# Value stages of two attention layers: spread values on ScalarE, half of the keys added on POOL, h added on TensorE

## The chip, the cores and the metric

The kernel runs on one NeuronCore of a Trainium2 chip. The metric is device time of one execution in microseconds (us). Engines are named as in the profile: PE is TensorE (PEld its weight loads), DVE is VectorE, ACT is ScalarE, POOL is GpSimd, SP is SyncE. All tensors here are float32.

## What is computed

A small vision tower over 128 images: patch embedding with window attention (9 patches and a class token), then attention, a mixture of experts, attention again, and a low-rank mixture. The change touches the two attentions. Cut to what matters, each is

```python
# x: layernorm(h); h is [128 images, 10 tokens, 256 channels], 16 heads of 16
q, k, v  = x @ Wq.T, x @ Wk.T, x @ Wv.T        # layer 0 with biases
scores   = einsum('bhqd,bhkd->bhqk', q, k) / 4
# layer 0: entries (0, 9) and (9, 0) set to -1e9; layer 1: clipped to +-10, then causal mask
weights  = softmax(scores)
out      = einsum('bhqk,bhkd->bhqd', weights, v)
h        = h + out @ Wo.T
```

So token t has `t + 1` keys in layer 1, and all 10 in layer 0.

## The kernel before

**Tiling.** The 128 images lie on the 128 partitions. A token is a tile `t` of 256 columns (T = 10, C = 256), so that attention runs inside a partition and none of it is a matmul between tokens. `h` holds 10 such tiles (`h_at(t)`). `a_qkv[:, t, :]` holds query, key and value of tile t, 256 columns each.

**Scores.** For each query the products with all keys are made by DVE or POOL and summed over 16 channels by DVE; ACT takes the exponent into `a_p`, with layout (query, head, key). `softmax_half` (DVE) divides: weights for POOL's queries stay in `a_p` (SBUF), those for DVE's queries go into a PSUM bank (`weight_bank`).

**The value stage**, once a layer. For each query t the values of n keys (`keys(layer, t)`: 10 in layer 0, t + 1 in layer 1) are multiplied with the weights and added over the keys. Queries are split by engine: `POOL_VALUES` (0, 2, 4, 6, 8 in layer 0; 0, 1, 2, 3, 4, 6, 8 in layer 1) and `DVE_VALUES` (the others).
- DVE's queries: `value_products` (line 1158) writes the products with the key innermost, n x 4 bytes apart from one channel to the next, from values that lie with the channel innermost; then a reduction over the last axis gives `a_o` (line 1469). TensorE turns `a_o` (`turn`, line 300).
- POOL's queries: `value_products` (the same line 1158) writes one row of 256 channels for each key into one of two slots (`pool_slot`). TensorE adds and turns them in one step: for each half of the channels, n matmuls with the unit matrix into one PSUM bank (line 1290). A matmul of float32 shows as two passes in the trace, so ten keys and two halves are 40.

ACT copies the turned result to SBUF (`a_oT`, line 1365). TensorE projects it with Wo (`project_o`, `mm_rows`, line 294, four passes), and DVE adds h (`add_o`, line 1485), then takes the statistics of the next layer norm (lines 347 and 349, and `veps`, line 354).

**Order of the work.** There is no planner: each engine has one instruction stream, and the order is the order in the source. Engines meet at counting semaphores. What matters here:
- PE: `turn_o(t)`, then `project_o(t - 1)`. `project_o(t)` waits for `a_h_made` of tile t - 1 (line 1305), since two banks alternate.
- DVE: products and sum of one of its queries, then `add_o` for the tiles up to t - 4, then the next query; at the end the remaining `add_o`. `add_o` waits for the projection.
- POOL: its queries in order; from the third on it waits until TensorE has turned the query two before in its list. After them come the reciprocal deviations (line 336) for the next stage.
- ACT: in layer 0 two exponents and then the copies `a_oT`; in layer 1 a loop over tiles that normalizes, copies the turned x (line 1323), copies queries, keys and values from PSUM (lines 1327, 1329) and takes the exponent of one query (`row_exponent`, line 1335).

Layer 0 is followed by the expert stage: `norm_rows` (line 364) normalizes h on ACT, TensorE turns it and computes the router's logits, and ranking, gathering and 27 expert slots follow, which TensorE fills. SP loads the experts' weights after the logits. Layer 1 is followed by the low-rank stage. No DMA is issued by the value stages.

## Time and profile before

| | us |
|---|---|
| median of 3 runs | 852.29 |
| lowest and highest | 847.16, 853.20 |
| the profiled execution, its own time | 849.13 |
| its span, first to last instruction | 847.4 |
| mean granted clock of TensorE in it | 0.931 |
| PE busy (4399 instructions) | 729.8, 86% |
| DVE busy | 535.9, 63% |
| POOL busy | 396.5, 47% |
| ACT busy | 358.6, 42% |

All times inside the kernel are of that one profiled execution, counted from the start of its span. In it the first value stage lies between about 430 and 489 us and the second between about 784 and 819. Busy shares are of the whole span; stages have different limits. The granted clock is a share of 2.4 GHz: 1.00 is the high of its two levels (2.4 GHz) and 0.50 the low one (1.2 GHz). An engine's idle time is followed by the one whose signal ended it. Durations of PE passes overlap with those of their neighbours, so a group's time is read from its first start to its last end.

### The profile page before, as it was taken

The page shows a single profiled execution, that of the slowest core. Times are in us where ns is not written, and L with a number is a line of the kernel's source. Part 1 is how long each engine was busy: PE and PEld are TensorE (multiplying, and loading weights), DVE is VectorE, ACT ScalarE, POOL GpSimd, SP SyncE. Part 2 cuts the span into 40 slices and gives each one's busy share as a digit, 9 for nine tenths or more (in the row PEclk, how much of TensorE's full clock was granted, in tenths as well). Part 3 has the DMA queues.
Part 4 walks back from the last instruction along what each step waited for, and adds up shares of the span by engine and source line. Part 5 has one row for each costly group of instructions (what it writes and reads, how often), then busy time and mean ns, then how long its engine had stood idle before and what let it go on. Part 6 is the DMA issues. An engine that isn't in the chain of part 4 may idle for free.

```text
span 847.4 us, 13115 instructions
## 1 busy us (share of the span) xinstructions
PE 729.8 (86%) x4399; PEld 630.6 (74%) x4399; DVE 535.9 (63%) x1253; ACT 358.6 (42%) x904; POOL 396.5 (47%) x272
## 2 busy tenths in 40 slices
PE   2879999999999999996846755999999999595668
PEld 2869998988989887553645754999999999354666
DVE  1578787777777777678999653222222223679956
ACT  3465666656656555532010131444444444162131
POOL 4565767667576661548564202333334332147410
PEclk9899999999999999999958865999999999597999
DMA  8532222222222020000020047799989980400001
GB/s 257 174 91 81 86 87 86 81 60 76 87 86 84 4 100 1 0 1 0 1 100 1 26 174 298 239 339 325 332 331 331 330 327 28 160 0 2 0 1 63
DMA packets 34489, 102.76 MB, mean 121 GB/s; under 512 B 3624, under 2 KB 12152, under 8 KB 27000
## 3 DMA queue, kind: packets, MB, share of 16 engines
q1 hardware_dynamic: 31832, 94.84, 32.6%
q0 software_dynamic: 2592, 7.10, 2.2%
q8 instruction: 36, 0.59, 0.3%
q14 instruction: 29, 0.24, 0.1%
HBM read 95.75 MB, written 6.17 MB: 120 GB/s over the span
## 4 chain that ended last, share of the span: by engine, by line
PE 69%; DVE 20%; POOL 3%; DMA 2%; issue 2%; ACT 1%; SPq 1%; POOLq 1%; DVEq 0%; ACTq 0%
PE banks L1581 12%; PE banks L1589 11%; PE banks L287 10%; PE banks L289 10%; PE banks L288 10%; PE banks L294 6%; PE banks L300 4%; DVE a_prod L1158 4%; PE banks L1260 4%; DVE a_o L1469 2%; DVE a_s L1393 2%; DVE banks L1393 1%; DVE w_raw L1402 1%; PE banks L1290 1%; PE banks L1919 1%
## 5 line engine op out<-in xcount | busy, mean ns | idle before, releaser
L401 POOL TENSOR_TENSOR x_lo<-xraw,x_hi 128x640 fp32r<-128x640 f32 x81 | 129.3, 1603 | 109.8 <-ACT x_hi L395 109.8
L287 PE MATMUL banks<-wc_hi,x_hi 128*128 128x256 f32 x405 | 121.9, 301 | 17.9 <-POOL x_lo L401 12.6
L1679 ACT ACTIVATE hid<-banks,b 128x128 f32<-128x128 f32 x216 | 79.3, 367 | 110.0 <-PE banks L1581 110.0
L288 PE MATMUL banks<-wc_lo,x_hi 128*128 128x256 f32 x405 | 116.5, 288 | 0.0
L289 PE MATMUL banks<-wc_hi,x_lo 128*128 128x256 f32 x405 | 116.4, 287 | 0.0
L287 PEld LDWEIGHTS banks<-wc_hi,x_hi 128*128 128x128 f32 x405 | 79.5, 196 | 20.4 <-issue 12.9
L1838 DVE TENSOR_TENSOR res<-banks,xb 128x256 f32<-128x256 f32 x27 | 11.5, 425 | 127.2 <-PE banks L1589 127.2
L288 PEld LDWEIGHTS banks<-wc_lo,x_hi 128*128 128x128 f32 x405 | 79.7, 197 | 1.8 <-issue 0.2
L289 PEld LDWEIGHTS banks<-wc_hi,x_lo 128*128 128x128 f32 x405 | 79.3, 196 | 0.0
L424 DVE BATCH_NORM_STATS2 stats<-banks 128x6 f32<-128x256 f32 x81 | 34.6, 427 | 69.7 <-ACT pe_sb L418 69.0
L418 ACT ACTIVATE pe_sb<-banks 128x256 f32<-128x256 f32 x81 | 31.0, 383 | 111.8 <-PE banks L289 111.8
L287 PE MATMUL banks<-wkv_hi,xg_hi 128*128 128x512 f32 x162 | 70.9, 438 | 4.4 <-DVE xg_lo L485 4.2
L1581 PEld LDWEIGHTS banks<-xT,w_raw 128*128 128x128 f32 x448 | 67.8, 196 | 5.8 <-ACT xT L1667 0.9
L1581 PE MATMUL banks<-xT,w_raw 128*128 128x128 f32 x448 | 69.6, 280 | 0.5 <-ACT xT L1667 0.5
L1717 POOL TENSOR_TENSOR y<-bve,mhalf 128x1 f32<-128x1 f32 x27 | 20.4, 755 | 104.9 <-DVE bve L1846 104.9
L1290 PE MATMUL banks<-ident,a_prod 128*128 128x128 f32 x324 | 46.5, 311 | 24.4 <-POOL a_prod L1158 24.4
L336 POOL TENSOR_TENSOR rstd<-veps,mhalf 128x5 f32<-128x5 f32 (+5 forms) x31 | 32.6, 1053 | 73.7 <-DVE veps L354 57.0
L1589 PE MATMUL banks<-w_raw,hid 128*128 128x256 f32 x224 | 66.9, 380 | 0.0
L1290 PEld LDWEIGHTS banks<-ident,a_prod 128*128 128x128 f32 x324 | 46.2, 227 | 25.9 <-issue 15.6
L1581 PEld LDWEIGHTS banks<-xT,w1more 128*128 128x128 f32 x416 | 61.8, 191 | 4.7
L289 PE MATMUL banks<-wkv_hi,xg_lo 128*128 128x512 f32 x162 | 64.5, 398 | 0.0
L288 PE MATMUL banks<-wkv_lo,xg_hi 128*128 128x512 f32 x162 | 63.9, 395 | 0.0
(298 smaller groups left out, 1778.5 us busy)
## 6 DMA issues: line engine op xcount, KB each, us to landing
w_raw<-in_w SPq DMA_DIRECT2D x28, 1024.0 KB, 6.7
xraw<-in_x_main SPq DMA_DIRECT2D x27, 768.0 KB
w1more<-in_w SPq DMA_DIRECT2D x13, 1024.0 KB, 5.8
w2more<-in_w SPq DMA_DIRECT2D x13, 1024.0 KB, 8.2
xraw<-in_x_rest SPq DMA_DIRECT2D x27, 114.0 KB
yl<-y_rows SPq DMA_DIRECT2D x2, 1028.0 KB, 7.1
a_w<-in_qkv_w SPq DMA_DIRECT2D x2, 768.0 KB, 5.4
x_rows<-w_raw SPq DMA_DIRECT2D x5, 256.0 KB, 2.0
```

The lines of the kernel that those rows point to most:

```text
L287: pe.matmul(dst, a[0], b[0], start=start, stop=False)
L288: pe.matmul(dst, a[0], b[1], start=False, stop=False)
L289: return pe.matmul(dst, a[1], b[0], start=False, stop=stop)
L294: last = pe.matmul(dst, aT[:, c * P:(c + 1) * P], w[:, c, a:b], start=(c == 0), stop=(c == CH - 1))
L300: last = pe.transpose(dst[:, c * P:(c + 1) * P], src[:, c * P:(c + 1) * P], ident[:, :])
L401: pool.tensor_tensor(x_lo[:, i % RING_X, :], xraw[:, k].rearrange("p c b -> p (c b)"), x_hi[:, i % RING_X, :], ALU.subtract).then_inc(sem( ...
L424: dve.bn_stats(stats[0][:, k, :], bank(i % 2)).then_inc(sem("stats_made0"), 1)
L1158: return eng.tensor_tensor(out, a_qkv[:, 0:n, 2 * C:3 * C].rearrange("p s (h d) -> p s h d", d=D16), key_weights(layer, t, n), ALU.mult)
L1290: last = pe.matmul(bank(t % 2, c * P, (c + 1) * P), slot[:, k * C + c * P:k * C + (c + 1) * P], ident[:, :], start=(k == 0), stop=(k == ns ...
L1581: last = pe.matmul(bank(fc % 2, 0, P), weights_of(s)[0][:, c * FF + fc * P:c * FF + (fc + 1) * P], xT[:, s % 2, c * P:(c + 1) * P], start= ...
L1589: last = pe.matmul(down_bank(s), hid[:, s % 2, fc, :], weights_of(s)[1][:, fc * C:(fc + 1) * C], start=(fc == 0), stop=(fc == FC - 1))
L1679: act.activation(hid[:, s % 2, fc, :], bank(fc % 2, 0, P), ACT.Gelu, bias=b1[:, bass.ds(e * FC + fc, 1)]).then_inc(sem("gelu_made"), 1)
```

## The change

- ACT gets a new piece of work, `spread_values`: it copies the values from `a_qkv` into `a_prod[:, 1, :]` with the key innermost (`values_by_channel`: channel c, key s at column 10 c + s). In layer 0 this is one copy of 2560 elements behind the two exponents, in layer 1 one of 256 elements for each tile, in the loop; there the exponents move one round later, and the last spread stands between the exponents of queries 8 and 7.
- DVE's products (`dve_values`) read values, and write products, both with the key innermost. DVE has one slot in place of two (`a_prod[:, 0]`) and waits for its own sum of the query before, and once for all spreads.
- POOL, where a query has more than five keys, adds the upper part of its rows to the lower part (`fold_pool_values`): ten keys leave five in layer 0; in layer 1 query 6 has seven and leaves four, query 8 has nine and leaves five. TensorE sums only what is left (`kept_keys`).
- `project_o` has a third matmul, unit matrix by `h_at(t)`, into the same bank. DVE's addition to h goes; ACT copies the bank into h (`copy_h(t - 1)` behind the copy of `a_oT` for tile t) and signals `a_h_made`.
- Two semaphores take over the counts of two others (`unfolded` those of `vprod_raw`, `consts_made` that of `a_p_cleared`).

The diff, cut to its core:

```diff
+        def pool_values(pool, layer, t):
             n = keys(layer, t)
+            p_t = a_p[:, t * T * H16:(t + 1) * T * H16].rearrange("p (h s) -> p s h", s=T)[:, 0:n, :]
+            return pool.tensor_tensor(pool_slot(layer, t)[:, 0:n * C].rearrange("p (s h d) -> p s h d", s=n, d=D16),
+                                      a_qkv[:, 0:n, 2 * C:3 * C].rearrange("p s (h d) -> p s h d", d=D16),
+                                      p_t.unsqueeze(3).broadcast_to([P, n, H16, D16]), ALU.mult)
+        def kept_keys(layer, t):
+            n = keys(layer, t)
+            return (n + 1) // 2 if n > HALF else n
+        def folded(layer, t):
+            return kept_keys(layer, t) < keys(layer, t)
+        def fold_pool_values(pool, layer, t):
+            n, m = keys(layer, t), kept_keys(layer, t)
+            slot = pool_slot(layer, t)
+            return pool.tensor_tensor(slot[:, 0:(n - m) * C], slot[:, 0:(n - m) * C], slot[:, m * C:n * C], ALU.add)
+        def values_by_channel(n=T):
+            return a_prod[:, 1, :].rearrange("p (c s) -> p c s", s=T)[:, :, 0:n]
+        def dve_values(dve, layer, t):
+            n = keys(layer, t)
+            i = [q for q in DVE_VALUES[layer] if q // HALF == t // HALF].index(t)
+            p_t = weight_bank(t // HALF, i * T * H16, (i + 1) * T * H16).rearrange("p (h s) -> p h s", s=T)[:, :, 0:n]
+            return dve.tensor_tensor(a_prod[:, 0, 0:n * C].rearrange("p (h d s) -> p h d s", h=H16, s=n),
+                                     values_by_channel(n).rearrange("p (h d) s -> p h d s", d=D16),
+                                     p_t.unsqueeze(2).broadcast_to([P, H16, D16, n]), ALU.mult)
...
+                if folded(layer, t):
+                    pool_values(pool, layer, t).then_inc(sem("unfolded"), 1)
+                    pool.wait_ge(sem("unfolded"), NW + 1 + made)
+                    fold_pool_values(pool, layer, t).then_inc(sem("a_pool_values_made"), 1)
+                else:
+                    pool_values(pool, layer, t).then_inc(sem("a_pool_values_made"), 1)
...
-                ns, slot = keys(layer, t), pool_slot(layer, t)
+                ns, slot = kept_keys(layer, t), pool_slot(layer, t)
...
-                mm_rows(pe, bank(6 + t % 2), a_oT[:, t % 2, :], wo, 0, C).then_inc(sem("a_o_done"), 1)
+                for c in range(CH):
+                    pe.matmul(bank(6 + t % 2), a_oT[:, t % 2, c * P:(c + 1) * P], wo[:, c, :], start=(c == 0), stop=False)
+                pe.matmul(bank(6 + t % 2), ident[:, :], h_at(t), start=False, stop=True).then_inc(sem("a_o_done"), 1)
...
+        def spread_values(act, layer, a, b):
+            act.wait_ge(sem("a_qkv_made"), seen(layer, "qkv_made", 2 * b))
+            act.activation(values_by_channel()[:, :, a:b].rearrange("p c s -> p s c"), a_qkv[:, a:b, 2 * C:3 * C], ACT.Copy)\
+               .then_inc(sem("a_values_spread"), 1)
+        def copy_h(act, layer, t):
+            act.wait_ge(sem("a_o_done"), seen(layer, "o_done", t + 1))
+            act.activation(h_at(t), bank(6 + t % 2), ACT.Copy).then_inc(sem("a_h_made"), 1)
...
                     if t:
                         copy_qkv(act, 1, t - 1)
-                    if t >= 4:
-                        row_exponent(act, SCORED[t - 4])
+                        spread_values(act, 1, t - 1, t)
+                    if t >= 5:
+                        row_exponent(act, SCORED[t - 5])
                 copy_qkv(act, 1, T - 1)
-                for t in SCORED[T - 4:]:
+                for t in SCORED[T - 5:T - 2]:
+                    row_exponent(act, t)
+                spread_values(act, 1, T - 1, T)
+                for t in SCORED[T - 2:]:
                     row_exponent(act, t)
...
+                spread_values(act, 0, 0, T)
...
                 act.activation(a_oT[:, t % 2, :], bank(t % 2), ACT.Copy).then_inc(sem("a_oT_made"), 1)
+                if t:
+                    copy_h(act, layer, t - 1)
                 if layer == 0 and t == 7:
                     norm_rows(act, 0)
+            copy_h(act, layer, T - 1)
...
+            dve.wait_ge(sem("a_values_spread"), 1 + T * layer)
             for i, t in enumerate(DVE_VALUES[layer]):
...
-            dve.wait_ge(sem("a_o_done"), seen(layer, "o_done", t + 1))
-            dve.tensor_tensor(h_at(t), bank(6 + t % 2), h_at(t), ALU.add).then_inc(sem("a_h_made"), 1)
             dve.wait_ge(sem("a_h_made"), seen(layer, "h_made", t + 1))
```

## Rows read from the trace of the kernel before

**Rows 1.** Time by stretch, value stages: us, busy time by engine, PEclk, DMA.

```profile
430.30:488.50 58.20, 40.93 (x256) 38.07 (x256) 51.17 (x48) 6.18 (x15) 25.76 (x7) 0.79 0.11 42
...
784.40:818.70 34.30, 21.95 (x143) 19.95 (x141) 28.30 (x41) 3.06 (x8) 12.47 (x5) 0.95 0.00 0
```

**Rows 2.** Chain that ended last, first value stage (start us, us, what).

```profile
433.56 4.76 DVE a_prod L1158
438.34 2.82 DVE a_o L1469
...
479.38 5.66 PE banks L1290 x40
...
488.57 0.92 ACT w_raw L364 x2
```

**Rows 3.** Waits of the first value stage (us in total, times, longest).

```profile
PE banks L294 <- DVE h L1485: 12.1, 3, 6.9
```

**Rows 4.** Groups of POOL by shape (xcount, busy us, mean ns, idle before).

```profile
L1158 POOL TENSOR_TENSOR a_prod<-a_qkv,a_p 128x2560 f32<-128x2560 f32 x5 | 23.7, 4755 | 20.3 <-PE banks L1290 15.2 <-DVE a_p L1435 5.0
...
L1117 POOL TENSOR_TENSOR a_prod<-a_qkv 128x1280 f32<-128x1280 f32 x1 | 2.9, 2905 | 0.0
...
L604 POOL TENSOR_TENSOR vprod<-vprod 128x1024 f32<-128x1024 f32 x10 | 24.0, 2400 | 0.7
```

**Rows 5.** Order of time, POOL and DVE, first value stage (start us, us).

```profile
430.39 9.46 POOL L1158 TENSOR_TENSOR a_prod<-a_qkv,a_p 128x2560 f32<-128x2560 f32 x2 [5.03 <-DVE a_p L1435]
...
464.61 4.75 POOL L1158 TENSOR_TENSOR a_prod<-a_qkv,a_p 128x2560 f32<-128x2560 f32 x1 [11.03 <-PE banks L1290]
...
467.69 1.69 DVE L354 TENSOR_SCALAR veps<-mv 128x4 f32<-128x4 f32 x1
```

**Rows 6.** Groups of DVE by shape, from 400 to 490 us.

```profile
L1158 DVE TENSOR_TENSOR a_prod<-a_qkv,banks 128x2560 f32<-128x2560 f32 x5 | 23.7, 4731 | 0.0
...
L1402 DVE TENSOR_TENSOR w_raw<-a_qkv,banks 128x2560 f32<-128x2560 f32 x1 | 2.8, 2820 | 0.0
```

**Rows 7.** Order of time, PE, first value stage.

```profile
435.26 7.34 PE L1290 MATMUL banks<-ident,a_prod 128*128 128x128 f32 x40 [15.32 <-POOL a_prod L1158]
...
444.05 4.63 PE L1290 MATMUL banks<-ident,a_prod 128*128 128x128 f32 x40
...
485.96 1.89 PE L294 MATMUL banks<-a_wo,a_oT 128*128 128x256 f32 x8
```

**Rows 8.** Groups of ACT by shape, whole run.

```profile
L1365 ACT ACTIVATE a_oT<-banks 128x256 f32<-128x256 f32 x20 | 7.6, 383 | 75.7 <-PE banks L1290 70.8 <-PE banks L300 4.9
...
L1335 ACT ACTIVATE a_p<-a_s 128x160 f32<-128x160 f32 x1 | 0.5, 489 | 4.6 <-DVE a_s L1388 4.6
...
L1335 ACT ACTIVATE a_p<-a_s 128x16 f32<-128x16 f32 x1 | 0.2, 233 | 0.0
```

**Rows 9.** Order of time, ACT, layer 1's query, key and value loop.

```profile
753.46 1.28 ACT L1335 ACT_TABLE_LOAD   x1
...
760.60 0.60 ACT L1327 ACTIVATE a_qkv<-banks 128x512 f32<-128x512 f32 x1 [0.67 <-PE banks L1260]
761.46 0.38 ACT L1329 ACTIVATE a_qkv<-banks 128x256 f32<-128x256 f32 x1 [0.27 <-PE banks L1260]
```

**Rows 10.** Chain that ended last, second value stage.

```profile
784.45 2.97 DVE a_prod L1158
...
808.33 4.02 PE banks L1290 x36
...
818.75 2.07 ACT z_xn L364 x4
```

**Rows 11.** Order of time, POOL, second value stage.

```profile
787.21 3.37 POOL L1158 TENSOR_TENSOR a_prod<-a_qkv,a_p 128x1792 f32<-128x1792 f32 x1 [0.17 <-PE banks L1290]
...
793.16 4.28 POOL L1158 TENSOR_TENSOR a_prod<-a_qkv,a_p 128x2304 f32<-128x2304 f32 x1 [2.58 <-PE banks L1290]
```

**Rows 12.** Time by stretch, two us with TensorE nearly idle.

```profile
787.00:789.00 2.00, 0.07 (x1) 0.00 (x0) 1.97 (x2) 0.38 (x1) 1.83 (x2) 1.00 0.00 0
```

More of the change, by code:

```diff
@@ L599, in value_prod @@
                                by_key(attn).unsqueeze(3).broadcast_to([P, NP, H8, DH8]), ALU.mult)\
-                .then_inc(sem("vprod_raw"), 1)
+                .then_inc(sem("unfolded"), 1)
         def fold_values(pool, n):
-            pool.wait_ge(sem("vprod_raw"), n + 1)
+            pool.wait_ge(sem("unfolded"), n + 1)
             pool.tensor_tensor(vprod[:, C:KEPT * C], vprod[:, C:KEPT * C], vprod[:, KEPT * C:], ALU.add).then_inc(sem("vprod_made"), 1)
@@ L1145, in score_place @@
                 "p h s -> p s h" if kind == "row" else "p s h -> p s h")
-        def key_weights(layer, t, n):
-            if t in DVE_VALUES[layer]:
-                i = [q for q in DVE_VALUES[layer] if q // HALF == t // HALF].index(t)
-                p_t = weight_bank(t // HALF, i * T * H16, (i + 1) * T * H16)
-            else:
-                p_t = a_p[:, t * T * H16:(t + 1) * T * H16]
-            return p_t.rearrange("p (h s) -> p s h", s=T)[:, 0:n, :].unsqueeze(3).broadcast_to([P, n, H16, D16])
@@ L1156, in value_products @@
-        def value_products(eng, layer, t, out):
-            n = keys(layer, t)
-            return eng.tensor_tensor(out, a_qkv[:, 0:n, 2 * C:3 * C].rearrange("p s (h d) -> p s h d", d=D16),
-                                     key_weights(layer, t, n), ALU.mult)
+        def pool_values(pool, layer, t):
+            n = keys(layer, t)
+            p_t = a_p[:, t * T * H16:(t + 1) * T * H16].rearrange("p (h s) -> p s h", s=T)[:, 0:n, :]
+            return pool.tensor_tensor(pool_slot(layer, t)[:, 0:n * C].rearrange("p (s h d) -> p s h d", s=n, d=D16),
+                                      a_qkv[:, 0:n, 2 * C:3 * C].rearrange("p s (h d) -> p s h d", d=D16),
+                                      p_t.unsqueeze(3).broadcast_to([P, n, H16, D16]), ALU.mult)
@@ L1177, in pool_slot @@
             return a_prod[:, 2 + POOL_VALUES[layer].index(t) % 2, :]
-        def dve_slot(layer, t):
-            return a_prod[:, DVE_VALUES[layer].index(t) % 2, :]
         def job_place(layer, i):
@@ L1205, in pool_attention @@
                 inverse_std(pool, *batch_of("attention 1", 0))
-                pool.memset(a_p[:, :], 0.0).then_inc(sem("a_p_cleared"), 1)
+                pool.memset(a_p[:, :], 0.0).then_inc(sem("consts_made"), 1)
                 inverse_std(pool, *batch_of("attention 1", 1))
@@ L1211, in pool_attention @@
             for i, t in enumerate(POOL_VALUES[layer]):
-                n = keys(layer, t)
                 pool.wait_ge(sem("a_p_made"), seen(layer, "p_made", 1 + t // HALF))
@@ L1215, in pool_attention @@
                     pool.wait_ge(sem("a_o_turned"), seen(layer, "o_turned", POOL_VALUES[layer][i - 2] + 1))
-                value_products(pool, layer, t, pool_slot(layer, t)[:, 0:n * C].rearrange("p (s h d) -> p s h d", s=n, d=D16))\
-                    .then_inc(sem("a_pool_values_made"), 1)
+                made = sum(folded(0, q) for q in POOL_VALUES[0]) * layer + sum(folded(layer, q) for q in POOL_VALUES[layer][:i + 1])
+                if folded(layer, t):
[4 more added lines that the diff above has]
+                    pool_values(pool, layer, t).then_inc(sem("a_pool_values_made"), 1)
             if layer == 0:
@@ L1329, in copy_qkv @@
             act.activation(a_qkv[:, t, 2 * C:3 * C], bank(5), ACT.Copy).then_inc(sem("a_qkv_made"), 1)
+        def spread_values(act, layer, a, b):
[5 more added lines that the diff above has]
+            act.activation(h_at(t), bank(6 + t % 2), ACT.Copy).then_inc(sem("a_h_made"), 1)
         def row_exponent(act, t):
-            act.wait_ge(sem("a_p_cleared"), 1)
+            act.wait_ge(sem("consts_made"), 5)
             act.wait_ge(sem("a_s_made"), seen(1, "s_made", SCORED.index(t) + 1))
@@ L1462, in dve_attention @@
             added = 0
+            dve.wait_ge(sem("a_values_spread"), 1 + T * layer)
             for i, t in enumerate(DVE_VALUES[layer]):
-                n, slot = keys(layer, t), dve_slot(layer, t)
-                by_key = slot[:, 0:n * C].rearrange("p (h d s) -> p s h d", s=n, d=D16)
-                if i >= 2:
-                    dve.wait_ge(sem("a_o_made"), len(DVE_VALUES[0]) * layer + i - 1)
-                link(value_products(dve, layer, t, by_key))
-                dve.tensor_reduce(a_o[:, t * C:(t + 1) * C], slot[:, 0:n * C].rearrange("p (c s) -> p c s", s=n), AX, ALU.add)\
+                n = keys(layer, t)
+                if i:
+                    dve.wait_ge(sem("a_o_made"), len(DVE_VALUES[0]) * layer + i)
+                link(dve_values(dve, layer, t))
+                dve.tensor_reduce(a_o[:, t * C:(t + 1) * C], a_prod[:, 0, 0:n * C].rearrange("p (c s) -> p c s", s=n), AX, ALU.add)\
                    .then_inc(sem("a_o_made"), 1)
```

## The prediction

> **What bounds the kernel now.** I first read the windows of the profile by stage, to see how full each engine is in the two value stages [rows 1]. In the first (58.2 us) DVE is busy 51.2, TensorE 40.9 and POOL only 25.8; in the second (34.3 us) DVE is busy 28.3 and POOL 12.5. Then I read the chain that ended last, to see which engine sets the end. In the first stage it is DVE without a gap: five times a product of 4.76 us and a sum of 2.82, with h additions and statistics between them, and only then TensorE's last forty passes (ended 485.04) and the tail to ACT's normalization at 488.57 [rows 2]. Third, the waits: TensorE waits 12.1 us in all for DVE's additions to h, since project_o(t) needs h(t-1) and the additions queue behind DVE's products [rows 3]. POOL waits in turn for TensorE (15.2 us before its products) to free a slot [rows 4]. So DVE is the bound, and the other two engines idle behind it.
>
> **The first value stage (layer 0), part by part.** POOL keeps its product of 4.76 us [rows 4] and gains a fold of five keys, 5 x 256 = 1280 elements. The trace has no such fold there. A POOL product of 1280 elements takes 2.905 us, and a POOL fold of 1024 takes 2.400, which scales to 3.0 [rows 4]; a fold for nothing is excluded, because both rows read two SBUF tensors at that rate. I take 2.95, and 7.75 a tile with the wait between the two. POOL starts at 430.39, as before [rows 5]. Five tiles without a stall end at 430.39 + 38.75 = 469.15. A stall is not due: the third tile needs the first slot back at 445.9, and the first tile is handed over at 438.15.
>
> DVE loses ten h additions. Its product should fall to the price of the score product, which also reads one SBUF and one PSUM tensor, writes in order and takes 2.82 us for the same 2560 elements, against 4.73 now [rows 6]. The bounds are 2.82 and 4.73; what is different about the old product is its output, written 40 bytes apart, so I take 2.82. DVE then needs about 5.65 us a tile and is ahead of POOL. Even at 4.73 its last tile would come at about 474, some 1 us after TensorE wants it.
>
> TensorE's sums halve, to twenty passes a tile. Forty took 4.63 us at the high clock (0.116 each) and 7.34 at the low one (0.184) [rows 7]. So the last sums start 0.15 after POOL and end at 469.15 + 0.15 + 2.3 = 471.6, in place of 485.04: 13.4 us earlier.
>
> The tail gets longer. project_o has six passes in place of four; eight took 1.89 us [rows 7], so 0.24 each, 1.4 a tile. From the end of the last sums to the end of project_o(9) it is now 3 x 1.4 = 4.2 us. Then ACT copies h (9) and turns x2(0), which are queued ahead of the normalization, 0.38 each with little overlap [rows 8]; with them and the hand-over it starts 4.85 after the sums. Before it started 488.57 - 485.04 = 3.53 after them [rows 2]. Loss 1.3. POOL's next reciprocal deviations wait for its last fold, until 469.15, and ACT's first four normalizations then end near 472.3, just before they would hold up the copy for tile 8. **Gain of the first stage: 13.4 - 1.3 = 12.1 us.**
>
> ACT's spread: its exponent writes 40 bytes apart too, 0.489 us for 160 elements and 0.233 for 16 [rows 8], so 1.78 ns an element. The spread of 2560 is then 0.2 + 4.55 = 4.75 us, and it starts behind the exponents, some 4.6 us before DVE's first product at 433.56 [rows 2]; the two come out even to within 0.2. Cost nothing: DVE is not the bound any more and has some 5 us to spare.
>
> One more wait moves. DVE's veps took 1.69 us, from 467.69 until 469.38, and POOL's product ended at 469.36 [rows 5]: DVE stood until POOL had let go. POOL is now busy without a break, so the veps after tile 3 may stand for a whole fold, up to 2.95 us. DVE's slack of 5 us hides it. The Trainium skill says on the page "SBUF — State Buffer", section "Who interferes with whom", that a DVE instruction in a two-port mode, or one with two SBUF inputs against a reading POOL instruction, blocks outright for that instruction; by this rule, the trace agrees on veps, and the sum stays as it is.
>
> **The second value stage (layer 1).** Two things differ. First, ten small spreads of 256 elements stand in ACT's loop for queries, keys and values, 0.2 + 240 x 1.78 ns = 0.66 us each. In a round ACT waits 0.67 and 0.27 us for TensorE [rows 9], 0.94 together, so a spread fits. But round 5 also has the table load of 1.28 us [rows 9], and 0.66 + 1.28 do not fit into 0.94: query 6, which DVE waits for, comes 1.0 us late (0 to 1.5). From there DVE is full, so the stage starts at 785.45 in place of 784.45 [rows 10].
>
> Second, only tiles 6 and 8 are folded (three and four keys). POOL's product of tile 6 began at 787.21, when TensorE had summed tile 3 [rows 11]; that is now 1.0 later for the start and 0.9 for two longer projections: 789.1. Then product 3.37 and fold 1.85, product 4.28 [rows 11] and fold 2.4 [rows 4], with hand-overs 12.1: 801.2. Twenty passes follow, to 803.6. Before, the thirty-six ended at 808.33 + 4.02 = 812.35 [rows 10], so 8.75 earlier. DVE (tiles 5, 7, 9 at 1.75 + 1.75, 2.3 + 2.3, 2.8 + 2.8, and six statistics) is done with tile 9 at 801.5, ahead. The tail up to ACT's normalization was 6.4 us [rows 10] and grows by only 0.2, since h(9) comes later but no addition queues in DVE. **Gain: 8.5 us.**
>
> Between and behind the stages nothing else changes, and the experts, which start from the routing, move forward with it. The renamed semaphores cost nothing.
>
> **Sum.** 12.1 + 8.5 = 20.6 us. The profiled execution took 849.13 us (span 847.4), which gives 828.5. I add 1.5 for TensorE at the low clock in parts where it was at the high one (0 to 11, below): 830.0. The median of the runs is 852.29, 3.2 above the profiled execution; against it 830 is 2.6% less. A difference of about 1% is what a measurement of this kernel can tell.
>
> **The rivals.** *TensorE falls to the low clock in both tails.* The mean was 0.79 of full speed in the first stage and 0.95 in the second [rows 1], and TensorE now has less to do. Then twenty passes cost 1.4 us more and 4.2 us of projections up to 4.2 more: 5.5 a stage, 11 in all, 839.5. Against it: its idle time before the last sums is some 2.4 and 2 us, and a stretch of 2 us with TensorE almost idle still shows 1.00 [rows 12], while the forty slow passes came after 15.3 us of idling [rows 7]. The Trainium skill, page "TensorE: Matmul & The Clock Gate", Part 1, holds that low is the default and that activity lifts it; the trace agrees in the slow passes after the long idle time, and by it this rival is what a thinner TensorE gets. Chance 0.15.
>
> *DVE's product stays at 4.7 us*, since the order of writing was not its cost. Tile 9 comes 1 to 2 us late in either stage: 833. Chance 0.06.
>
> *POOL and DVE shut each other out.* If the new DVE product held what POOL reads through, 5 x 2.82 = 14 us would go onto POOL's path in the first stage and 5 in the second: a loss of 2 and a gain of 3.4, 848. Against it: POOL's products take 4.755 us on average beside DVE's present ones [rows 4], and the new one has its weights in PSUM as well. Chance 0.03.
>
> *Slower: the spread is dear on ACT.* Say s us for 256 elements. In layer 1 ten of them stretch the loop by 10(s - 0.9); in layer 0 the one spread takes 10s, and above s = 1.3 DVE's last tile is late by 10s - 13.2. Gains of 20.6 (with the 1.0 in it) are used up at s = 2.2, and s = 3 gives about 866. The exponent's rows give 0.66 [rows 8]. Chance 0.03.
>
> **How the numbers follow.** The forecast, POOL as the pace of both stages, has 0.73 and a range of its own of 824 to 836 (the runs of before lie 6 us apart; the fold is 2.9 to 3.0, the late query 0 to 1.5, the clock 0 to 5). With the clock rival whole the range is 822 to 840. Faster by over 1% (below 843.8): 0.73 + 0.15 + 0.06 = 0.94, less 0.02 for what I have not seen, 0.92. Within 1%: 0.05. Slower: 0.03.
>
> **What would show it.** After: POOL in the first stage busy 38 us without a gap, folds of 2.9 us; DVE products of 2.8 us; the last sums ending 38 to 42 us after POOL's first product; no wait of TensorE for h; the wait that ends last before TensorE's sums is POOL's. Each spread of 256 at 0.66 us, and the value stage of layer 1 starting about 1 us later behind its loop. The forecast is wrong if POOL's products become longer beside the folds, if the passes of the tails take 0.18 us and more, or if POOL waits for TensorE again.

## The result and the profile after

| | before | after |
|---|---|---|
| median, us | 850.87 (4 runs, 847.16 to 853.20) | 828.34 (4 runs, 827.10 to 829.73) |
| ratio, 95% interval | | 0.9745 [0.9718, 0.9771] |
| profiled execution | 849.13 | 829.73 |
| its span | 847.4 | 827.6 |
| mean granted clock | 0.931 | 0.938 |

The changed kernel is 2.5% faster. The forecast was 830.0 with a range of 822 to 840. The kernel before has one run more here than ahead of the prediction, which moved its median from 852.29 to 850.87. Its profiled execution lies 1.7 us below that median, the one of the changed kernel 1.4 above its own, so that the profiles differ by 19.4 us and the medians by 22.5.

**Where the 19.8 us of the span lie.** I cut both profiles at the same instructions. Each number is the difference of two starts.

| stretch | before | after | change | forecast |
|---|---|---|---|---|
| start of the span to POOL's first value product | 430.39 | 431.40 | +1.01 | 0 |
| layer 0: to ACT's second group of normalizations for the expert stage | 58.18 | 45.78 | -12.40 | -12.1 |
| routing: to DVE's comparison that opens the expert slots | 18.54 | 16.79 | -1.75 | 0 |
| experts: to DVE's first addition to h | 225.36 | 225.67 | +0.31 | 0 |
| to DVE's score product of query 6, layer 1 | 28.83 | 29.90 | +1.07 | +1.0 |
| to DVE's first value product of layer 1 | 23.15 | 23.15 | 0 | 0 |
| layer 1: to ACT's first normalization of the low-rank stage | 34.30 | 25.93 | -8.37 | -9.5 |
| rest | 28.65 | 28.98 | +0.33 | 0 |
| span | 847.40 | 827.60 | -19.80 | -20.6, and 1.5 allowed for the clock |

The 8.5 us that the prediction gives for layer 1 are these 9.5 less the 1.0 of query 6.

The windows of the changed kernel by stage (us, then the busy time of PE, PEld, DVE, ACT and POOL, the granted clock, DMA) answer to [rows 1]:

```profile
431.40:477.20 45.80, 31.69 (x176) 27.91 (x176) 37.45 (x38) 12.60 (x27) 40.08 (x12) 0.81 0.13 52
772.70:798.60 25.90, 22.25 (x145) 19.97 (x143) 19.62 (x30) 6.59 (x18) 16.62 (x7) 1.00 0.00 1
```

POOL, busy 25.8 of 58.2 us before, is busy 40.1 of 45.8 in the first stage. The waits of the changed kernel from 430 to 489 us (us in total, times, longest) answer to [rows 3]:

```profile
PE banks L1310 <- POOL a_prod L1165: 24.5, 5, 18.3
...
DVE a_prod L1175 <- ACT a_prod L1356: 0.2, 1, 0.2
```

TensorE's wait for DVE's additions to h (12.1 us before) has no line any more. TensorE now waits for POOL's fold in front of each of its five sums, and DVE waits 0.2 us in all for ACT's spread. The groups of the same stretch by shape (xcount, busy us, mean ns) answer to [rows 4] and [rows 6]:

```profile
L1150 POOL TENSOR_TENSOR a_prod<-a_qkv,a_p 128x2560 f32<-128x2560 f32 x5 | 23.8, 4758 | 5.0 <-DVE a_p L1475 5.0
...
L1165 POOL TENSOR_TENSOR a_prod<-a_prod 128x1280 f32<-128x1280 f32 x5 | 14.5, 2893 | 0.4
...
L1175 DVE TENSOR_TENSOR a_prod<-a_prod,banks 128x2560 f32<-128x2560 f32 x5 | 14.1, 2812 | 0.2 <-ACT a_prod L1356 0.2
...
L1356 ACT ACTIVATE a_prod<-a_qkv 128x2560 f32<-128x2560 f32 x1 | 4.8, 4759 | 0.0
```

DVE's product fell from 4731 to 2812 ns, and POOL's stayed as it was beside it (4755, now 4758). In order of time (start, us), the changed kernel's first stage shows the new path, POOL and then TensorE and then ACT:

```profile
431.40 4.76 POOL L1150 TENSOR_TENSOR a_prod<-a_qkv,a_p 128x2560 f32<-128x2560 f32 x1 [5.02 <-DVE a_p L1475]
...
459.30 2.89 POOL L1165 TENSOR_TENSOR a_prod<-a_prod 128x1280 f32<-128x1280 f32 x1
...
461.20 1.01 DVE L354 TENSOR_SCALAR veps<-mv 128x4 f32<-128x4 f32 x1
...
466.99 2.88 POOL L1165 TENSOR_TENSOR a_prod<-a_prod 128x1280 f32<-128x1280 f32 x1
...
470.02 2.47 PE L1310 MATMUL banks<-ident,a_prod 128*128 128x128 f32 x20 [2.40 <-POOL a_prod L1165]
472.32 1.03 PE L1327 MATMUL banks<-a_wo,a_oT 128*128 128x256 f32 x4
...
471.09 2.08 ACT L364 ACTIVATE w_raw<-h,nmr,rstd 128x256 f32<-128x256 f32 x4 [3.05 <-DVE nmr L341]
473.07 0.36 ACT L1402 ACTIVATE a_oT<-banks 128x256 f32<-128x256 f32 x1
...
477.18 2.07 ACT L364 ACTIVATE w_raw<-h,nmr,rstd 128x256 f32<-128x256 f32 x4
```

POOL's last fold ends at 469.87, 38.47 us after its first start: 7.69 a query. The last sums end at 472.49, 41.09 after it, and ACT's second group starts 4.69 later. In layer 1 the changed kernel's order of time shows the one place that the forecast had not in it:

```profile
770.04 2.07 PE L1327 MATMUL banks<-a_wo,a_oT 128*128 128x256 f32 x4
771.91 1.06 PE L1328 MATMUL banks<-h,ident 128*128 128x256 f32 x2
...
774.50 2.47 POOL L1150 TENSOR_TENSOR a_prod<-a_qkv,a_p 128x1280 f32<-128x1280 f32 x1 [2.35 <-PE banks L1310]
```

The first projection runs at the low clock (2.07 and 1.06 us, later 1.03 and 0.59), and POOL waits 2.35 us for the slot that TensorE sums behind it.

### The profile page after: what moved, and what is told of

The parts are those of the page before. It is cut to its first block, busy times and chain, and to the rows that moved or that the text cites. A ratio compares the mean times of both kernels' runs of the same rounds, so it can differ in the third digit from the quotient of the medians.

```text
span 827.6 us, 12959 instructions
## 1 busy us (share of the span) xinstructions
PE 720.0 (87%) x4311; PEld 618.7 (75%) x4311; DVE 513.3 (62%) x1233; ACT 375.7 (45%) x935; POOL 414.6 (50%) x279
## 4 chain that ended last, share of the span: by engine, by line
PE 71%; DVE 12%; POOL 9%; DMA 2%; ACT 2%; issue 2%; SPq 1%; POOLq 1%; DVEq 0%; ACTq 0%
PE banks L1619 12%; PE banks L1627 11%; PE banks L287 10%; PE banks L289 10%; PE banks L288 10%; PE banks L294 5%; PE banks L300 4%; POOL a_prod L1150 3%; PE banks L1280 2%; POOL a_prod L1165 2%; PE banks L1310 2%; DVE a_s L1433 2%; DVE w_raw L1442 1%; PE banks L1957 1%; DVE banks L1433 1%
## 5 line engine op out<-in xcount | busy, mean ns | idle before, releaser
L287 PEld LDWEIGHTS banks<-wc_hi,x_hi 128*128 128x128 f32 x405 | 79.6, 196 | 21.1 <-issue 13.6
L1619 PE MATMUL banks<-xT,w1more 128*128 128x128 f32 x416 | 63.2, 274 | 0.0
L1280 PE MATMUL banks<-a_w,a_xT 128*128 128x512 f32 (+1 forms) x160 | 61.5, 519 | 0.4 <-DVE w_raw L1442 0.3
L1627 PE MATMUL banks<-w2more,hid 128*128 128x256 f32 x208 | 61.6, 380 | 0.0
```

What stands on the lines that cost most here:

```text
L287: pe.matmul(dst, a[0], b[0], start=start, stop=False)
L1280: last = pe.matmul(dst, a_xT[:, t % 2, c * P:(c + 1) * P], a_w[layer][:, c, a:b], start=(layer == 1 and c == 0), stop=(c == CH - 1))
L1619: last = pe.matmul(bank(fc % 2, 0, P), weights_of(s)[0][:, c * FF + fc * P:c * FF + (fc + 1) * P], xT[:, s % 2, c * P:(c + 1) * P], start= ...
L1627: last = pe.matmul(down_bank(s), hid[:, s % 2, fc, :], weights_of(s)[1][:, fc * C:(fc + 1) * C], start=(fc == 0), stop=(fc == FC - 1))
```

## The experiments

**The theory** is that of the prediction: DVE was the bound, each part of the change takes work off DVE or TensorE until POOL paces the stage, and the parts share one path. **The rival** is that each part is worth its own busy time, so that their gains add. A second question, which the first kernels opened, is what the fold of layer 0 is worth, and why the slow product costs the stage more than the prediction said. The ratios compare each kernel with runs of the kernel before on the same chip; times are medians in us. The medians of the kernel before were 851.03 beside the three kernels without one part and the first with late spreads, 850.89 beside the parts alone, 853.02 beside the repeat of the changed kernel and the three with another fold or none in layer 0, and 850.00 beside the last row. Medians of different sets can thus differ by 1 to 3 us for no reason of the kernels; the ratios are free of that.

| kernel | median | ratio, 95% | layer 0 stage | routing | to query 6 | layer 1 stage |
|---|---|---|---|---|---|---|
| before | 850.87 | | 58.18 | 18.54 | 28.83 | 34.30 |
| changed | 828.34 | 0.9745 [0.9718, 0.9771] | 45.78 | 16.79 | 29.90 | 25.93 |
| changed, once more | 828.49 | 0.9730 [0.9698, 0.9762] | 45.73 | 16.82 | 29.88 | 24.52 |
| without the spread | 832.19 | 0.9777 [0.9740, 0.9814] | 52.25 | 19.22 | 28.84 | 26.62 |
| without h on TensorE | 833.78 | 0.9795 [0.9757, 0.9832] | 44.60 | 18.59 | 29.92 | 30.54 |
| without the folds | 830.94 | 0.9756 [0.9716, 0.9795] | 45.19 | 19.24 | 29.90 | 26.09 |
| spreads of layer 1 late | 827.03 | 0.9728 [0.9686, 0.9770] | 45.76 | 16.95 | 28.83 | 24.97 |
| the spread alone | 833.72 | 0.9805 [0.9786, 0.9824] | 48.16 | 18.68 | 29.91 | 29.58 |
| h on TensorE alone | 837.30 | 0.9853 [0.9832, 0.9874] | 52.27 | 19.28 | 28.81 | 26.75 |
| the folds alone | 847.53 | 0.9965 [0.9945, 0.9984] | 56.19 | 17.14 | 28.81 | 35.32 |
| fold of three keys in layer 0 | 824.96 | 0.9671 [0.9645, 0.9696] | 43.26 | 17.39 | 29.88 | 25.57 |
| the same, spreads late | 825.91 | 0.9692 [0.9669, 0.9715] | 43.25 | 17.35 | 28.82 | 24.61 |
| no fold in layer 0, spreads late | 827.87 | 0.9712 [0.9687, 0.9737] | 45.10 | 19.33 | 28.81 | 25.93 |
| without the spread, one normalization moved | 831.23 | 0.9791 [0.9757, 0.9825] | 48.35 | 18.80 | 28.82 | 26.59 |

The stretches are those of the table above, each from the one profiled execution of its kernel.

### 1. Without the spread

```diff
-            return dve.tensor_tensor(a_prod[:, 0, 0:n * C].rearrange("p (h d s) -> p h d s", h=H16, s=n),
-                                     values_by_channel(n).rearrange("p (h d) s -> p h d s", d=D16),
-                                     p_t.unsqueeze(2).broadcast_to([P, H16, D16, n]), ALU.mult)
+            slot = a_prod[:, i_of(layer, t) % 2, :]
+            return dve.tensor_tensor(slot[:, 0:n * C].rearrange("p (h d s) -> p s h d", s=n, d=D16),
+                                     a_qkv[:, 0:n, 2 * C:3 * C].rearrange("p s (h d) -> p s h d", d=D16),
+                                     p_t.rearrange("p h s -> p s h").unsqueeze(3).broadcast_to([P, n, H16, D16]), ALU.mult)
...
-                spread_values(act, 0, 0, T)
```

In layer 1 the loop of ACT is that of the kernel before as well, and DVE has its two slots again.

> The changed kernel with ACT's spread taken out: DVE's products read the values with the channel innermost and write 40 bytes apart again; folds on POOL and h on TensorE stay. Theory (POOL sets layer 0, and DVE has slack): DVE's product is 4.7 us again in place of 2.8, yet layer 0 gets only 0.5 to 1.5 us longer, and layer 1 1 us shorter because queries are no longer late behind spreads; 828.5 in all, within 1 us of the changed kernel. Rival (DVE's products still lie on the path): five times 1.9 in layer 0 and 4.7 in layer 1, 12 to 14 us slower, about 841.

Measured: 832.19, 3.9 above the changed kernel, so neither the theory (828.5) nor the rival (841). In layer 1 query 6 comes 1.06 us earlier, as expected. The layer 0 stage of its profiled execution takes 52.25, 6.5 more in place of 0.5 to 1.5. Order of time in it, TensorE, ACT and DVE:

```profile
474.46 0.41 PE L300 MATMUL banks<-ident,a_o 128*128 128x128 f32 x2 [0.98 <-DVE a_o L1507]
477.34 2.07 PE L1331 MATMUL banks<-a_wo,a_oT 128*128 128x256 f32 x4 [2.47 <-ACT a_oT L1401]
...
474.95 2.07 ACT L364 ACTIVATE w_raw<-h,nmr,rstd 128x256 f32<-128x256 f32 x4 [7.14 <-DVE nmr L341]
476.93 0.36 ACT L1401 ACTIVATE a_oT<-banks 128x256 f32<-128x256 f32 x1
...
457.94 4.74 DVE L1176 TENSOR_TENSOR a_prod<-a_qkv,banks 128x2560 f32<-128x2560 f32 x1
...
471.50 2.82 DVE L1507 TENSOR_REDUCE a_o<-a_prod 128x256 f32<-128x2560 f32 x1
...
474.78 0.13 DVE L341 SCALAR_TENSOR_TENSOR nmr<-mv,rstd 128x4 f32<-128x4 f32 x1
```

DVE's last query is 0.98 us late for TensorE, as the prediction had it. What it left out is ACT's queue. `norm_rows` for the first four tiles stands in ACT's queue ahead of the copy for tile 8. It needs a small operation (`nmr`) that DVE does only behind its last query, here at 474.78. So ACT stands for 7.14 us, copies tile 8 at 476.93 instead of behind TensorE's sums, and TensorE waits another 2.47 us and comes back at the low clock (2.07 us for four passes).

This profiled execution, at 839.02, is the slowest of the six of this kernel (830.41 the fastest), and no other of them has a trace. That its stage is the typical one is therefore not shown by this kernel. But the kernel with h on TensorE alone (section 5), which has the same slow product, shows the same rows in a profiled execution of 836.76 beside a median of 837.30:

```profile
475.35 2.07 PE L1331 MATMUL banks<-a_wo,a_oT 128*128 128x256 f32 x4 [2.47 <-ACT a_oT L1401]
...
472.96 2.07 ACT L364 ACTIVATE w_raw<-h,nmr,rstd 128x256 f32<-128x256 f32 x4 [7.14 <-DVE nmr L341]
```

### 2. Without the spread, and ACT's normalization one tile later

```diff
-                if layer == 0 and t == 7:
+                if layer == 0 and t == 8:
                     norm_rows(act, 0)
```

> The kernel with ACT's spread taken out, and besides ACT's first four normalizations for the experts in layer 0 (norm_rows(0)) moved from behind the copies for tile 7 to behind those for tile 8. Without the move the stage of layer 0 took 52.25 us, 6.5 more than with the spread, where 0.5 to 1.5 had been expected. Theory: DVE's slow products make its last query late by some 2 us only, but the normalizations wait for a value that DVE makes behind that query, and ACT's copy for tile 8 stands behind them; with the move TensorE's projection of tile 8 no longer waits for them, and the stage takes 48 to 49 us; 828 to 829 in all. Rival (the late last query alone costs the 6.5): 52, 832.

Measured: stage 48.35, 3.9 shorter than in experiment 1. In order of time, TensorE and ACT:

```profile
472.58 1.03 PE L1331 MATMUL banks<-a_wo,a_oT 128*128 128x256 f32 x4
...
475.21 1.13 PE L1331 MATMUL banks<-a_wo,a_oT 128*128 128x256 f32 x4 [1.18 <-ACT a_oT L1401]
...
472.82 2.07 ACT L364 ACTIVATE w_raw<-h,nmr,rstd 128x256 f32<-128x256 f32 x4 [0.97 <-DVE nmr L341]
```

Tile 8's copy is out of the way and the passes are fast again. Of the 3.9 us the clock makes up about 2.6: in experiment 1 the projections of tiles 8 and 9 take 5.27 us together (477.34 to 482.61), here about 2.7 without the wait between them. The other 1.3 is TensorE's shorter wait for ACT. What is left of it stands before tile 9 (1.18 us). Of the remaining 2.6 us over the changed kernel nearly all are the late query (0.90 us of waiting) and this wait. The stage came out as expected (48 to 49), and the rival's 52 did not. The total did not: 831.23 in place of 828 to 829. The medians, 832.19 and 831.23, can't tell the two kernels apart; the queue is shown by the rows, its worth in the total is not.

### 3. Without h on TensorE

```diff
-                for c in range(CH):
-                    pe.matmul(bank(6 + t % 2), a_oT[:, t % 2, c * P:(c + 1) * P], wo[:, c, :], start=(c == 0), stop=False)
-                pe.matmul(bank(6 + t % 2), ident[:, :], h_at(t), start=False, stop=True).then_inc(sem("a_o_done"), 1)
+                mm_rows(pe, bank(6 + t % 2), a_oT[:, t % 2, :], wo, 0, C).then_inc(sem("a_o_done"), 1)
...
-                    copy_h(act, layer, t - 1)
...
+            dve.tensor_tensor(h_at(t), bank(6 + t % 2), h_at(t), ALU.add).then_inc(sem("a_h_made"), 1)
```

> The changed kernel with h added by DVE again, after the projection; no third matmul in the projection and no copy of h on ACT. Theory: with fast products DVE adds h early enough in layer 0, and the tail is 1.3 us shorter, so layer 0 stays within 1 us; in layer 1 the additions of h(4) and h(5) queue behind DVE's last query and hold TensorE's last sums back by 3 to 4 us; 830 to 831 in all. Rival (the 20 additions of 0.42 us count in full): 9 us slower, 837.

Measured: 833.78, 5.4 above the changed kernel, some 3 more than I expected. Layer 0 is 1.2 us *shorter* than in the changed kernel (44.60), since its tail has four passes a projection again; layer 1 is 4.6 longer. Order of time of TensorE in layer 1:

```profile
790.41 2.04 PE L294 MATMUL banks<-a_wo,a_oT 128*128 128x256 f32 x4 [3.59 <-DVE h L1520]
792.25 4.24 PE L1310 MATMUL banks<-ident,a_prod 128*128 128x128 f32 x20
```

The addition to h stands behind DVE's product and sum of tile 9. TensorE waits 3.59 us and then runs at the low clock: the projection takes 2.04 instead of 1.03, and the twenty passes 4.24 instead of 2.47. I had expected the last sums 3 to 4 us late in layer 1 and had not counted the clock, which makes up 2.8 us of the 4.6. Another 1.8 us of the total lie in the routing (18.59 in place of 16.79), for which I had no term either. So this part pays in layer 1 and costs 1.2 us in layer 0.

### 4. Without the folds

```diff
-            return (n + 1) // 2 if n > HALF else n
+            return n
```

> The changed kernel without POOL's folds; TensorE sums all keys again. Theory: TensorE then sets both stages, about 8.0 us for two tiles in layer 0 against POOL's 7.7 with folds, plus 2.3 for the longer last sums: layer 0 longer by 3 to 5 us, layer 1 by 2, 833 to 835 in all. Rival (folding made POOL the bound and costs more than it saves): as fast or faster, 826 to 828.

Measured: 830.94, with an interval that overlaps the changed kernel's. I had expected 833 to 835 and a layer 0 stage longer by 3 to 5 us. It takes 45.19, not longer than with folds (45.78), which is what the rival says of this stage; its total (826 to 828) is not met either. Order of time in it:

```profile
456.42 4.76 POOL L1150 TENSOR_TENSOR a_prod<-a_qkv,a_p 128x2560 f32<-128x2560 f32 x1 [2.52 <-PE banks L1310]
...
458.93 4.63 PE L1310 MATMUL banks<-ident,a_prod 128*128 128x128 f32 x40
...
466.20 4.63 PE L1310 MATMUL banks<-ident,a_prod 128*128 128x128 f32 x40
...
480.21 0.86 PE L294 MATMUL banks<-w_rt,w_raw 128*128 128x8 f32 x4
```

Without folds TensorE paces the stage: its forty passes start every 7.27 us (458.93 and 466.20), and POOL waits for it three times, 7.1 us in all. With folds POOL paces it, at 7.69 a query. Once the other two parts are in, a fold of five keys moves the bound from TensorE to POOL without lowering it. What this kernel loses lies behind the stage, in the routing (19.24 against 16.8), where its logits run at the low clock; section 8 comes back to that.

### 5. One part alone

The edits are those of experiments 1, 3 and 4, two at a time (with its addition to h on DVE, say, and without folds, the spread alone is left).

The spread alone:

> The kernel before with only ACT's spread and DVE's quick products; no folds, h added by DVE. Theory (the parts stand in for each other: whichever frees DVE frees TensorE's wait for h): DVE needs 5.65 us a query in layer 0 and TensorE becomes the bound with 4.6 of sums and 2.1 of projections for two tiles: layer 0 shorter by 9 to 11 us, layer 1 by 2 to 4; 838 to 840 in all. Rival (each part brings its own busy time, 15 us of products): 836.

h on TensorE alone:

> The kernel before with only h moved to TensorE and ACT; products of 4.7 us on DVE, no folds. Theory: TensorE no longer waits for DVE, and both need about 8 us for two tiles in layer 0: shorter by 8 to 10 us there, by 3 to 4 in layer 1; 838 to 841. Rival (each part brings its own busy time, 20 additions of 0.42 us): 8 us, 842.5.

The folds alone:

> The kernel before with only POOL's folds. Theory: DVE stays the bound, since TensorE still waits for its additions to h; only the last sums are shorter, by 2 to 3 us in layer 0 and 1.9 in layer 1: 846. Rival (halved sums count in full, 128 passes of 0.116 us): 15 us, 836.

Measured: 833.72, 837.30 and 847.53, so gains of 17.2, 13.6 and 3.4 us against 850.89. The sizes that I expected for single parts were off. The spread brought 4 to 6 us more than the theory said (838 to 840), and even more than the rival (836); h on TensorE came out 0.7 below its range (838 to 841), with 5.9 us in layer 0 where 8 to 10 were expected and 7.5 in layer 1 in place of 3 to 4; the folds brought 1.5 less than expected (846).

What the three answer is whether gains add. They add up to 34, and all three together give 22.5. Taken away one at a time from the changed kernel, they cost 3.9, 5.4 and 2.6 by the medians, in all 11.9; by the ratios it is 2.7, 4.3 and 0.9, in all 8, and each of these three intervals overlaps the changed kernel's. So the cost of a single part in the changed kernel isn't clear of the noise, while the 34 against 22.5 are.

The rival, gains that add, falls: the spread and h on TensorE stand in for each other. Either ends much of the same wait, TensorE's for DVE's additions. Over both stages it is 20.9 us before, 9.3 with the spread alone and nothing with h on TensorE. The folds alone don't shorten it, as the waits of that kernel in layer 0 show (us in total, times, longest), beside [rows 3]:

```profile
PE banks L294 <- DVE h L1518: 17.4, 3, 7.4
```

TensorE is ready earlier and waits 17.4 us in place of 12.1, since DVE is still the bound. Nor do the folds shorten the layer 0 stage where the slow product stays and h is on TensorE: 52.27 without them, 52.25 with them. Both hold the queue of experiment 1 in their tails, which hides a part of what h on TensorE gives by itself in layer 0.

### 6. The spreads of layer 1 out of the loop

```diff
-                        spread_values(act, 1, t - 1, t)
...
-                for t in SCORED[T - 5:T - 2]:
+                for t in SCORED[T - 5:T - 3]:
                     row_exponent(act, t)
-                spread_values(act, 1, T - 1, T)
-                for t in SCORED[T - 2:]:
+                spread_values(act, 1, 0, T)
+                for t in SCORED[T - 3:]:
```

> The changed kernel with the ten spreads of layer 1 put together into one copy of 2560 elements, between the exponents of queries 5 and 8, where ACT waits for DVE. Theory (table load and spreads together made query 6 late by 1.1 us): the value stage of layer 1 starts 1.1 us earlier behind its loop, 827.2. Rival (the lateness has another cause, or one large spread holds up the exponent of query 8): no change or up to 1 us slower, 828.3 to 829.3.

Measured: the stretch up to query 6 is 28.83, exactly as before and 1.07 less than changed, so the small spreads in ACT's loop cost what the prediction said, and one spread of 2560 elements behind the loop costs that stretch nothing. The total, 827.03, is 1.3 lower, as expected (827.2), with overlapping intervals.

### 7. A fold of three keys in layer 0

```diff
-            return (n + 1) // 2 if n > HALF else n
+            return 7 if layer == 0 else (n + 1) // 2 if n > HALF else n
```

> The changed kernel with a smaller fold in layer 0: POOL adds three keys of ten and TensorE sums seven (28 passes); layer 1 as it is. Theory (POOL sets layer 0 at 7.7 us a query, TensorE needs only 5.7 for two tokens): POOL 6.6 and TensorE 6.5, about even; the last sums end 37.5 us after POOL's first product in place of 41.1, and the stage is 3.3 us shorter; 825. Rival (sums and projections of TensorE at the low clock set the stage): no gain, 828 to 830.

Measured: 824.96, where 825 was expected. Its interval [0.9645, 0.9696] ends just below that of the changed kernel on the same chip, [0.9698, 0.9762]; this is the fastest kernel of the study by the medians. POOL needs 6.62 us a query, TensorE has 28 passes, and the last sums end 36.60 us after POOL's first start, 4.5 earlier than in the changed kernel. The stage is only 2.5 shorter, where 3.3 were expected. Order of time, where the other 2 us went:

```profile
456.94 4.75 POOL L1150 TENSOR_TENSOR a_prod<-a_qkv,a_p 128x2560 f32<-128x2560 f32 x1
...
458.65 3.07 DVE L354 TENSOR_SCALAR veps<-mv 128x4 f32<-128x4 f32 x1
461.63 2.81 DVE L1175 TENSOR_TENSOR a_prod<-a_prod,banks 128x2560 f32<-128x2560 f32 x1
...
467.93 2.07 ACT L364 ACTIVATE w_raw<-h,nmr,rstd 128x256 f32<-128x256 f32 x4 [4.20 <-DVE nmr L341]
469.91 0.36 ACT L1402 ACTIVATE a_oT<-banks 128x256 f32<-128x256 f32 x1
...
470.32 1.13 PE L1327 MATMUL banks<-a_wo,a_oT 128*128 128x256 f32 x4 [1.71 <-ACT a_oT L1402]
```

An operation on four elements takes 3.07 us, until POOL's product ends (461.69). DVE's last query is late by that, then `nmr`, then ACT's normalization with tile 8's copy queued behind it, and TensorE waits 1.71 us. It is the queue of experiment 1 again. With the spreads of layer 1 late besides:

> Both: three keys folded in layer 0, and the ten spreads of layer 1 as one copy between the exponents of queries 5 and 8. Theory: the two gains lie in different stages and add, 3.3 + 1.1, and 1 more where TensorE's clock is high at layer 1's first projection: 823 to 824. Rival: what is won in one stage is given back behind it, 826 or more.

Measured: 825.91, in place of 823 to 824. It can't be told from 824.96. The loop is 1.06 shorter (28.82), as in experiment 6, and the total doesn't show it. The same comparison with no fold in layer 0:

> One late spread in layer 1 and folds in layer 1 only; in layer 0 TensorE sums all ten keys (40 passes). Against the kernel with three keys folded it tells what the fold in layer 0 is worth. Theory: TensorE sets layer 0 at 8.0 us for two tokens, its last sums end 40.5 us after POOL's first product, and the stage takes 45.2; 2.5 us more than with three keys folded: 826 to 827. Rival (folding is worth nothing in any size): 823 to 824.

Measured: 827.87 (826 to 827 expected), 2.0 above the fold of three with late spreads, with overlapping intervals. So three keys beat five: clearly in the stage (43.26 and 43.25 against 45.73 to 45.78), in the total by a margin that just clears the noise. With late spreads the same comparison, 825.91 against 827.03 on another chip, leaves overlapping intervals. Against none the rows favour three (43.25 against 45.10 in the stage), the medians don't decide.

### 8. The changed kernel once more

> The changed kernel once more, for what differs between two profiles of one kernel. Theory: the three stretches of the change come out as in its first profile to 0.1 us (45.8 us from POOL's first product of layer 0 to ACT's second group of normalizations; 29.9 from the expert stage's first addition to query 6 in layer 1; 25.9 or 25.0 for layer 1's value stage, by TensorE's clock at its first projection), while what lies before the stage varies by some us and the routing, by the clock of the logits, between 16.8 and 19.2. Rival: the routing stays at 16.8, so that a short routing belongs to this kernel and is a gain of the change.

Measured: 828.49. The routing took 16.82 us, after 16.79, so the rival holds, and its shortening isn't one execution's luck; the kernel with late spreads, whose code up to there is the same, took 16.95. Kernels with another order of events just before it stand at 17.1 to 19.3 (table). The stretch before the value stage, where the code is the same in all kernels, lay between 428.3 and 431.4 and is the noise of such profiles. The layer 1 stage took 24.52, not 25.93. In order of time it shows why:

```profile
766.71 1.13 PE L1327 MATMUL banks<-a_wo,a_oT 128*128 128x256 f32 x4
767.68 0.60 PE L1328 MATMUL banks<-h,ident 128*128 128x256 f32 x2
...
769.76 2.47 POOL L1150 TENSOR_TENSOR a_prod<-a_qkv,a_p 128x1280 f32<-128x1280 f32 x1 [0.93 <-PE banks L1310]
```

The first projection is at the high clock here, and POOL waits 0.93 us for its slot in place of 2.35. These 1.4 us differ between two executions of one kernel.

## Why the prediction was right, and where it was not

**The bound.** POOL paces the first stage, as forecast: 38.47 us without a stall (38.75), a fold of 2.893 (2.95), the last sums 41.09 after its first start (41.2). No wait of TensorE for h is left.

**DVE's product.** Forecast 2.82, measured 2.812; of the two bounds, 2.82 and 4.73, the lower was right. The old form is what cost the time: in the kernel without the spread the product takes 4.74 again (457.94 to 462.68). That it was the order of writing is argued and not shown, since the order in which the weights are read changed with it.

**The tail of layer 0** took 4.69 (4.85), and the six passes of a projection 1.30 (472.32 to 473.62), 1.4 forecast. The loss of 1.3 was the right size: without h on TensorE the tail is 1.2 shorter.

**ACT's spreads** took 4.76 (4.75) and 0.66 to 0.67 (0.66). DVE waited 0.17 us for the large one, inside the 0.2 stated. In layer 1 query 6 came 1.07 late (1.0). Experiment 6 ties this to the spreads.

**The wait for POOL's instruction.** Bounded at 2.95, the veps after tile 3 took 1.01, from 461.20 to 462.21, and POOL's fold ended at 462.19. DVE's slack hid it, as said. In the fold of three keys the same operation took 3.07 and it did cost the stage time. The Trainium skill, page "SBUF — State Buffer", section "Who interferes with whom", has DVE and POOL exclude each other on their shared port pair for a whole instruction; the ends that coincide agree with it, here even for four elements.

**Layer 1** was 1.1 us short: 9.5 forecast, 8.4 in the profile, 9.8 in the second one of the same kernel. The term that was off is POOL's start of query 6, which I had put behind two longer projections at the high clock, 3.65 us after DVE's first value product (789.1 less 785.45). In the first profile the first of these projections ran at the low one, and POOL started 4.89 after it (777.58 less 772.69), in the second 3.48.

**The clock.** The allowance of 1.5 us was for passes that slow down. In the profile this took about 1.4 in layer 1, and the routing gave 1.75 back, so the two cancel, and the sum without allowance, 828.5, is nearer the median than 830.0. I had forecast nothing for the routing. That 830.0 stands next to the 829.73 of the profiled execution is in part luck: 1.1 us short in layer 1, 1.75 won in the routing, 1.0 of noise ahead of the stage and 0.6 in the experts and the rest against an allowance of 1.5. So is the nearness to the median, since the sum starts from a profiled execution that was 1.7 us faster than the median before. The rival of slow tails (839.5) fell: both last projections of layer 0 took 1.03 and 0.59 us. The waits before the last sums, 2.40 and 1.32 us, were as short as the prediction held against it.

**The step that was wrong** is the cover of DVE's slack: "Even at 4.73 its last tile would come at about 474, some 1 us after TensorE wants it", and its rival of 833 us. The late tile was 0.98 us, but its profiled stage was 6.5 longer. I looked for who waits for DVE's `a_o` and not for who waits for the small `nmr` behind it: ACT does, with tile 8's copy queued behind that wait. TensorE waits another 2.47 us for this copy and comes out of it at the low clock (2.07 us for four passes). The prediction had this queue in view where POOL's reciprocal deviations come late ("just before they would hold up the copy for tile 8"), and not where DVE does. The median of 832.19 is near the rival's figure, yet by more than that one term. The cover was thinner than the "some 5 us to spare": in the changed kernel DVE waits 2.54 us for POOL's reciprocal deviations ahead of `nmr`, and that is all a late last query can use up before ACT's queue moves.

```profile
470.89 0.17 DVE L341 SCALAR_TENSOR_TENSOR nmr<-mv,rstd 128x4 f32<-128x4 f32 x1 [2.54 <-POOL rstd L336]
```

**What I did not ask** is what the fold would be worth once the other two parts are in. The total holds without the answer, but experiment 4 shows that in layer 0 it was worth nothing by itself (POOL 7.69 us a query, TensorE without folds 7.27), and experiment 7 that a smaller one gives another 3.5 us by the medians of one chip.

## What to carry to other kernels

Parts of a change that free the same wait stand in for each other: cost each with the others in place, and not only against the kernel before. When work moves from one engine to another on the same path, weigh their times for one step: of the three sizes of fold tried here, the one that brings the two nearest to each other gave the shortest stage. And when an engine off the path gets late, follow everything behind it in its own queue, the small operations too, to whatever waits for them at the head of another engine's queue.

## What the runs showed of the hardware that I had not expected

**TensorE's clock fell and stayed low while it was nearly always busy.** In the routing TensorE turns tiles and does short passes of 8 columns. Four of them take 0.51 us at the high clock and 0.86 at the low one. The windows of ten us over the routing, first of the kernel before, then of the changed kernel:

```profile
490.00:500.00 10.00, 8.87 (x48) 8.77 (x48) 2.64 (x28) 4.62 (x13) 0.53 (x1) 0.60 0.21 79
```

```profile
478.00:488.00 10.00, 7.36 (x50) 6.93 (x48) 3.63 (x36) 5.06 (x14) 0.67 (x1) 0.74 0.26 86
```

Before, TensorE is busy 8.87 of 10 us and its granted clock is 0.60. Its last idle gap, 1.54 us, ended at 490.97, the passes stayed fast until 492.1, and from there to 499.8 they are slow, though no gap stands between them. Slow passes also fill more of the time, so the busy share is partly the clock's own doing. The Trainium skill, page "TensorE: Matmul & The Clock Gate", Part 1, holds that low is the default and that activity lifts the clock; a TensorE that is busy by the profile for 8.87 of 10 us at a mean of 0.60 does not agree with it as it stands. Whether the gap of 1.54 us ahead of the fall has a part in it, no run shows. Why one kernel keeps the high clock for longer than another (16.8 us of routing against 19.2) stays open: it repeated for the changed kernel, but no run isolates what sets it.

**A tiny DVE operation can wait for a whole POOL instruction.** The veps of four elements took 0.17 us where POOL was idle and 1.01, 1.69 and 3.07 us where POOL was in the middle of a fold or a product, each time until that instruction's end. The traces of the other kernels show no exception.

**A wait can cost more than its length.** After 3.59 us of waiting TensorE lost another 2.8 to the low clock (experiment 3), and after 2.47 about 2.6 (experiment 1), while waits of 1.71 and 1.18 us were followed by passes near the high clock (four in 1.13). Waits of 2.4 us went both ways in the changed kernel: twenty passes took 3.86 us behind 2.41 in the third query and 2.47 behind 2.40 in the last.
